# The first adapter's share of x: added to x tile by tile, instead of multiplied through W

## The reference

```
x1  = x  + (x @ B0[id0].T) @ A0[id0].T                      # first adapter
out = x1 + x1 @ W.T + b + 2 * ((x1 @ A1[id1]) @ B1[id1])    # base layer and second adapter
```

## Time and profile before

| what | value |
|---|---|
| median of 3 runs | 1397.52 us |
| profiled execution | 1398.88 us, its span 1396.9 us |
| TensorE busy | 1372.8 us, 98% |
| VectorE busy | 943.6 us, 68% |
| ScalarE busy | 529.1 us, 38% |
| moved by DMA | 311.6 MB, mean 223 GB/s |
| mean granted clock | 0.997 |

### The profile page before, as it was taken

The page is one execution under the profiler, slowest core; times in us unless marked ns, Lnnn a source line. Parts: engine busy times, 40 slices in busy tenths (PEclk is TensorE's granted clock), DMA queues, the critical chain, the costliest instruction groups (busy, mean ns, idle before and its releaser), DMA issues.

```text
span 1396.9 us, 16200 instructions
## 1 busy us (share of the span) xinstructions
PE 1372.8 (98%) x6024; PEld 1128.8 (81%) x6024; DVE 943.6 (68%) x1049; ACT 529.1 (38%) x588; POOL 79.1 (6%) x163
## 2 busy tenths in 40 slices
PE   6899999999999999999999999999999999999999
PEld 5788877888888878888888888888888888888887
DVE  4677897777877887687765566665755566665662
ACT  3444444433334443343324453333233444333321
POOL 2012010001010000001001000000101000000000
PEclk9999999999999999999999999999999999999999
DMA  9789764778888987599895335455856343555642
GB/s 343 242 293 306 264 238 147 243 236 282 297 292 307 314 297 264 178 301 327 287 358 194 110 112 180 163 175 168 276 204 189 117 135 134 169 167 189 194 151 83
DMA packets 98591, 311.60 MB, mean 223 GB/s; under 512 B 13009, under 2 KB 14289, under 8 KB 98513
## 3 DMA queue, kind: packets, MB, share of 16 engines
q1 hardware_dynamic: 92736, 298.96, 63.1%
q0 software_dynamic: 5776, 11.61, 2.9%
HBM read 254.94 MB, written 55.57 MB: 222 GB/s over the span
## 4 chain that ended last, share of the span: by engine, by line
PE 91%; DVE 4%; DMA 2%; issue 1%; ACT 1%; SPq 1%; ACTq 0%; DVEq 0%
PE acc L590 27%; PE acc L591 27%; PE acc L592 27%; DMA w_two<-w 2%; PE acc L565 2%; PE down_ps L549 2%; PE down_ps L550 2%; PE image_ps L535 1%; PE image_ps L529 1%; PE image_ps L530 1%; DVE w_one L759 1%; DVE bg_lo L794 1%; DVE w_lo L767 1%; DVE x_lo L789 0%; ACT w_hi L627 0%
## 5 line engine op out<-in xcount | busy, mean ns | idle before, releaser
L590 PE MATMUL acc<-x_hi,w_hi 128*128 128x512 f32 x1792 | 702.1, 392 | 16.3 <-DVE x_lo L789 12.5
L591 PE MATMUL acc<-x_lo,w_hi 128*128 128x512 f32 x1792 | 699.5, 390 | 0.0
L592 PE MATMUL acc<-x_hi,w_lo 128*128 128x512 f32 x1792 | 699.1, 390 | 0.0
L627 ACT ACTIVATE w_hi<-w_one 128x1024 fp32r<-128x1024 f32 x223 | 235.9, 1058 | 541.1 <-PE acc L592 504.5
L767 DVE TENSOR_TENSOR w_lo<-w_one,w_hi 128x1024 fp32r<-128x1024 f32 x223 | 273.1, 1225 | 215.2 <-ACT w_hi L627 215.2
L590 PEld LDWEIGHTS acc<-x_hi,w_hi 128*128 128x128 f32 x1792 | 337.6, 188 | 89.0 <-issue 16.6
L591 PEld LDWEIGHTS acc<-x_lo,w_hi 128*128 128x128 f32 x1792 | 337.6, 188 | 71.7 <-issue 1.0
L592 PEld LDWEIGHTS acc<-x_hi,w_lo 128*128 128x128 f32 x1792 | 337.3, 188 | 71.2
L660 ACT ACTIVATE sums<-acc 128x512 f32<-128x512 f32 x96 | 57.1, 594 | 203.7 <-PE acc L592 188.1
L826 DVE SCALAR_TENSOR_TENSOR sums<-acc,bias_sb,sums 128x512 f32<-128x512 f32 x128 | 95.7, 747 | 22.0 <-PE acc L565 20.8
L759 DVE TENSOR_TENSOR w_one<-w_one,w_two 128x1024 f32<-128x1024 f32 x79 | 96.4, 1220 | 17.1 <-DMA w_two<-w 17.1
(11 more groups left out here) (61 smaller groups left out, 610.3 us busy)
## 6 DMA issues: line engine op xcount, KB each, us to landing
w_one<-w SPq DMA_DIRECT2D x143, 512.0 KB, 5.5
w_one<-w_sums SPq DMA_DIRECT2D x80, 512.0 KB, 3.7
w_two<-w SPq DMA_DIRECT2D x79, 512.0 KB, 7.4
x_stage<-x SPq DMA_DIRECT2D x64, 512.0 KB, 4.4
out<-sums SPq DMA_DIRECT2D x128, 256.0 KB, 4.6
w_sums<-w_one SPq DMA_DIRECT2D x40, 512.0 KB, 4.1
resident<-x SPq DMA_DIRECT2D x32, 512.0 KB, 8.6
bg_raw<-w_rows SPq DMA_DIRECT2D x32, 512.0 KB, 5.0
```

What stands on the lines that cost most here:

```text
L590: pe.matmul(ps[:, :], w_hi[ws][:, c, :], hi, start=(c == 0), stop=False)
L591: pe.matmul(ps[:, :], w_hi[ws][:, c, :], lo, start=False, stop=False)
L592: mm = pe.matmul(ps[:, :], w_lo[ws][:, c, :], hi, start=False, stop=(c == H - 1))
L627: act.activation(w_hi[s % W_PARTS][:, :, :], w_one[s % W_ONES][:, :, :], ACT.Copy).then_inc(w_hi_ready, 1)
```

## The change

The image of W goes. In its place x1 = x + A0·(B0·x) is formed tile by tile, and all seven products work on x1.
- `project_down(d)`: B0·x and A1·x of a sample, as before, but in halves of a chunk (128 x 512) with three small buffers. Sample 1's eight chunks stand ahead of step 0, and sample 0's in steps 0 to 2. Those of the next group lie in products 4 and 5 of the group before.
- `project_up(v)`: two matmuls of 96 rows, with A0's columns (`up_w`, loaded and split by `load_up` and `split_up`) against `rank_x`, into two PSUM banks.
- `add_up(v)`: VectorE adds the banks to a chunk of x. Half of the chunks are in `resident`. The others are loaded to `bg_raw`, added, stored to a DRAM tensor `x1`, and read from there as operands.
- The product of A1, A0 and b1 is still needed for the second adapter, as its down part is taken of x and not of x1. Four matmuls with `across` (`make_image`, steps 6 to 9) form it.

The core of the diff (ScalarE's start has the order of VectorE's; lines left out are marked):

```diff
+def sum_at(p):
+    if p == 1:
+        return (5, 5, 6, 7)
+    return {1: (2, 3, 5, 6), 2: (2, 3, 6, 7)}.get(p % PRODUCTS, (1, 3, 5, 6))
...
+def downs(s):
     if s >= STEPS:
         return []
+    if s < 3:
+        first = (0, 8, 10, 13, 16)
+        return list(range(first[s + 1], first[s + 2]))
     g, i, o = where(s)
...
+    if g + 1 < GROUPS and H * 4 <= s % PER_GROUP < H * 5:
+        return [16 * (g + 1) + o]
+    if g + 1 < GROUPS and H * 5 < s % PER_GROUP <= H * 6:
+        return [16 * (g + 1) + 8 + s % PER_GROUP - H * 5 - 1]
+    return []
+def ups(s):
+    if s >= STEPS:
+        return []
+    if s < 0:
+        return [0, 1]
+    g, i, o = where(s)
+    found = [2, 3] if s == 0 else []
+    if i == 0:
+        found += [16 * g + 4 * A0 + r for r, at in enumerate((1, 2, 4, 5) if g else (4, 4, 5, 5)) if at == o]
+    found += [16 * g + 4 * B0 + r for r, at in enumerate((7, 8, 10, 11)) if at == s % PER_GROUP]
+    if i == 2:
+        found += [16 * g + 4 * A1 + r for r, at in enumerate((1, 3, 5, 7)) if at == o]
+    if i == 6 and g + 1 < GROUPS:
+        found += [16 * (g + 1) + r for r, at in enumerate((2, 4, 5, 6)) if at == o]
+    return found
...
+RANK_X_AT = {s + (1 if n < 2 else 2): n for s, n in LAST.items()}
...
+UP_SPLIT = {2: 1}
+UP_LOAD = {}
+for _g in range(GROUPS):
+    _s = PER_GROUP * _g
+    if _g:
+        UP_LOAD[_s - 15], UP_SPLIT[_s - 12] = 4 * _g + B1, 4 * _g + B1
+        UP_LOAD[_s - 7], UP_SPLIT[_s - 1] = 4 * _g + A0, 4 * _g + A0
+    UP_LOAD[_s + (3 if _g == 0 else 0)], UP_SPLIT[_s + 6] = 4 * _g + B0, 4 * _g + B0
+    UP_LOAD[_s + 7], UP_SPLIT[_s + 12] = 4 * _g + A1, 4 * _g + A1
+DOWN_AFTER = ((1, 3, 5), (5, 6))
+IMAGE_STEP = 6
...
+        up_w = sb("up_w", [96, D // 2], F32R)
+        rank_x = [sb(f"rank_x{k}", [96, T], F32R) for k in range(3)]
...
+        up_ps = [bank(f"up_ps{k}") for k in range(2)]
+        image_ps = bank("image_ps")
...
-                source = x_chunk(2 * g + 1, 0, r) if i < 4 else x_chunk(2 * g, 1, r)
+                y = RAW["up", 16 * g + 4 * (B0 if i < 4 else A1) + r]
+                sp.wait_ge(x1_stored[y % 2], DMA * raw_stores(y))
+                source = x1[2 * g + (i < 4)][:, 2 * r:2 * r + 2, :]
...
+            def load_raw(kind, number):
+                y = RAW[kind, number]
+                if y >= 2:
+                    before, one = RAW_AT[y - 2]
+                    if before == "down":
+                        sp.wait_ge(bg_ready, 2 * one + 2)
+                    else:
+                        sp.wait_ge(x1_stored[y % 2], DMA * raw_stores(y - 2))
...
+            def store_x1(v):
+                y = RAW["up", v]
+                n, half, r = up_chunk(v)
+                sp.wait_ge(up_added, 2 * v + 2)
+                sp.dma_start(x1[n][:, 2 * r:2 * r + 2, :], bg_raw[y % 2][:, :, :]).then_inc(x1_stored[y % 2], DMA)
...
+            for d in (0, 1):
+                load_raw("down", d)
+            for d in (2, 3):
+                load_early(d)
...
+            sp.wait_ge(ids_loaded, 2 * DMA)
+            sp.dma_start(down_raw[0][:, :, :], adapter(0, 1, b0).rearrange("u p c r -> (u p) c r")).then_inc(first_down_loaded, DMA)
+            sp.dma_start(down_raw[1][:, :, :], adapter(1, 1, a1).rearrange("u p c r -> (u p) c r")).then_inc(first_down_loaded, DMA)
+            for r in range(CH):
                 load_resident(0, 1, r)
+            sp.dma_start(identity_sb[:, :], identity).then_inc(identity_loaded, DMA)
+            load_w(0)
             load_w(1)
+            for r in range(CH):
+                load_resident(0, 0, r)
+            for d in (12, 13):
+                load_raw("down", d)
             load_w(2)
-            for r in range(2):
-                load_resident(0, 0, r)
+            keep_sum(0)
+            for d in (14, 15):
+                load_early(d)
...
+                for v in ups(s - 1) if s else ():
+                    if not up_resident(v):
+                        store_x1(v)
...
+                if s in (1, 2):
+                    for n in range(4 * s - 4, 4 * s):
+                        sp.dma_start(a1_raw[:, n, :, :], adapter(1, n, a1).rearrange("u p c r -> (u p) c r"))\
...
+                for v in ups(s + 1):
+                    if not up_resident(v):
+                        load_raw("up", v)
+                if s + 2 >= CH:
+                    for d in downs(s + 2):
+                        load_raw("down", d)
...
+            def project_down(d):
+                n, k = down_chunk(d)
                 if k == 0:
                     pe.wait_ge(down_ready, turn(n) + 1)
                     if turn(n):
                         pe.wait_ge(down_added, turn(n))
                 for u in range(2):
+                    pe.wait_ge(bg_ready, 2 * d + u + 1)
                     c = 2 * k + u
+                    hi, lo = down_parts(2 * d + u)
                     weights = down[:, c, :, :, :].rearrange("p h l r -> p (h l r)")
-                    pe.matmul(down_ps[:, :], weights, hi[:, u, :], start=(c == 0), stop=False)
-                    mm = pe.matmul(down_ps[:, :], weights, lo[:, u, :], start=False, stop=(c == C - 1))
-                mm.then_inc(bg_used, 1)
+                    pe.matmul(down_ps[:, :], weights, hi, start=(c == 0), stop=False)
+                    pe.matmul(down_ps[:, :], weights, lo, start=False, stop=(c == C - 1)).then_inc(bg_used, 1)
+            def project_up(v):
+                n, half, r = up_chunk(v)
+                if r == 0:
+                    pe.wait_ge(up_ready, v // 4 + 1)
+                    pe.wait_ge(rank_x_ready, turn(n) + 1)
+                for u in range(2):
+                    e = 2 * v + u
+                    if e >= 2:
+                        pe.wait_ge(up_added, e - 1)
+                    o = 2 * r + u
+                    pe.matmul(up_ps[e % 2][:, :], up_w[:, P * o:P * (o + 1)], rank_x_of(n)[:, :], start=True, stop=True)\
+                      .then_inc(up_done, 1)
+            def make_image(j):
+                pe.wait_ge(across_ready, 1)
+                pe.wait_ge(b1_rows_loaded, NB * DMA)
+                if j:
+                    pe.wait_ge(image_ready, j)
+                pe.matmul(image_ps[:, :], across, rows[:, T * j:T * (j + 1)], start=True, stop=True).then_inc(image_done, 1)
...
+                    if c == 1 and len(us) > 0:
+                        project_up(us[0])
                     if c == 3 and s >= 1:
                         add_rank(s - 1)
-                    if c == 5 and len(zs) > 1:
-                        multiply_chunk(zs[1])
-                    if c == 6 and len(zs) > 2:
-                        multiply_chunk(zs[2])
+                    if c == 3 and len(us) > 1:
+                        project_up(us[1])
+                    if c in DOWN_AFTER[s == 0]:
+                        k = DOWN_AFTER[s == 0].index(c)
+                        if k < len(ds):
+                            project_down(ds[k])
+                    if c == 6 and 0 <= s - IMAGE_STEP < 4:
+                        make_image(s - IMAGE_STEP)
+            for d in downs(-1):
+                project_down(d)
+            for v in ups(-1):
+                project_up(v)
...
+            def split_chunk(d):
+                wait_for_down_source(act, d)
+                for e in (2 * d, 2 * d + 1):
+                    if e >= 11:
+                        act.wait_ge(bg_used, e - 2)
+                    act.activation(down_parts(e)[0], down_source(e), ACT.Copy).then_inc(bg_hi_ready, 1)
+            def split_up(m):
+                act.wait_ge(up_loaded, 3 * DMA * (m + 1))
+                if m:
+                    act.wait_ge(up_done, 8 * m)
                 else:
...
+                    act.wait_ge(zeros_ready, 1)
+                for row in (0, 4 * R):
+                    act.activation(up_w[row:row + R, :], rank_raw[row:row + R, :], ACT.Copy)
+                act.activation(up_w[2 * R:3 * R, :], rank_raw[2 * R:3 * R, :], ACT.Copy).then_inc(up_hi_ready, 1)
...
+                    dve.wait_ge(up_added, up_number(p, r))
+                    if g == 0:
+                        dve.wait_ge(bg_ready, 32)
...
+            def split_chunk(d):
+                for e in (2 * d, 2 * d + 1):
+                    hi, lo = down_parts(e)
+                    dve.wait_ge(bg_hi_ready, e + 1)
+                    dve.tensor_tensor(lo, down_source(e), f32(hi), ALU.subtract).then_inc(bg_ready, 1)
...
+            def add_up(v):
+                n, half, r = up_chunk(v)
+                if up_resident(v):
+                    dve.wait_ge(resident_loaded[n % 2][r], DMA * (n // 2 + 1))
+                    chunk = resident[n % 2][:, 2 * r:2 * r + 2, :]
+                else:
+                    y = RAW["up", v]
+                    dve.wait_ge(bg_loaded[y % 2], DMA * raw_loads(y))
+                    chunk = bg_raw[y % 2][:, :, :]
+                for u in range(2):
+                    dve.wait_ge(up_done, 2 * v + u + 1)
```

(74 more changed lines are left out.)

402 lines of the change are left out of this document (168 added, 234 removed).

## The result

The changed kernel takes 1415.66 us (median of 4 runs, 1414.24 to 1420.35) against 1397.38: a ratio of 1.013 (95% interval 1.010 to 1.0161), 18.3 us slower. The profiled execution of it is the longest of the four, 1420.35, so its account adds up to more: a span of 1418.7 against 1396.9, +21.8. A second profile, of a run of 1412.27, is used where the two differ.

A forecast was written before the change was run, and what follows sets the result against it. TensorE, busy 98% of the span, was taken as the bound. Terms -15.3 + 22.1 + 2.3 - 3.2 + 4 + 4 = +13.9 on the profiled 1398.9 gave 1412.8, 1411 as a median; range 1396 to 1424.

The forecast's parts named there:

- TensorE's work: Whole kernel: image matmuls of 43.5 and 3.8 us go, up matmuls of 32.0 come: -15.3 us.
- start: Ahead of step 1: step 0 needs all of x[1] first; step 1 starts at 54, 37.5 lost for 15.4: +22.1 us.
- steps 1 to 16: TensorE waits for VectorE in steps 4, 5, 7 and 8: 10.2 us lost against 7.9, +2.3.
- product 2 and 3 of group 0: Forecast for product 2 of group 0: its chunks go, and their losses with them: -3.2 us.
- transfers, group 1: Product 1 of group 1: 18.9 MB in 45 us ask for about 420 GB/s, so W lags: +4 us, bounds 0 and +12.
- clock: Waits at the start and in steps 4 and 7 drop TensorE to 1.2 GHz: +4 us, bounds 0 and +9.
- One sign: Start: VectorE is busy without a gap from W(0)'s landing at about 20.
- The rival of a start held by transfers alone: Start +12, step 1 near 44, no new waits or clock and transfer costs: 1383 to 1390 us, chance 0.12.
- Steps 4 to 8: TensorE waits for up additions in steps 4 and 5 (3.9, 1.3), for image copies in 7 and 8 (3.7, 1.3).
- Its ceiling: Group 1, product 1: transfers capped at product 6's 354 GB/s, so 18.9 MB take 53.4 us, a lag of 8.4.
- lighter stretches follow: Group 1, behind product 1: asking for W ahead absorbs 3.5 us of the 8.4 lag, and lighter stretches come next.
- The rule of the Trainium skill: Each of five waits (start, steps 4, 5, 7, 8) costs 3.4 us, 17 for 4: 1424, chance 0.06.

The follow-up runs named there:

- The start's order: Changed kernel with VectorE and ScalarE splitting all eight chunks of x[1] before W(0), and add_up between x_hi and x_lo: 1410.83 us.
- the run with the clock held up: Changed kernel with extra matmuls of zeros in TensorE's waits at the start, in step 0 and in step 4: 1414.37 us.
- the queue order: Changed kernel with the image copy right behind w_lo in VectorE's list, and in steps 4 and 5 the first add_up there too: 1407.97 us.
- the second timing: The changed kernel as it is, timed again beside the kernel before: 1414.31 us, ratio 1.0114.

## Why the prediction was right

| term of the sum | predicted | profile after | second profile |
|---|---|---|---|
| TensorE's work | -15.3 | -15.5 | -15.4 |
| start | +22.1 | +25.3 | +24.2 |
| steps 1 to 16 | +2.3 | +4.3 | +3.1 |
| product 2 and 3 of group 0 | -3.2 | -3.2 | -3.2 |
| transfers, group 1 | +4 | +10.9 | +5.0 |
| clock | +4 | in the start and steps 1 to 16 | same |

The lost time before is 15.4 at the start, 7.9 in steps 1 to 16 and 2.4 in group 1; each entry but the first is the loss after less that. TensorE's work is what the other rows leave of +21.8 and of +13.7 (span 1410.6).

- **TensorE's work** came as counted: 5928 records for 6024, steps of 5.44 or 5.69 plus 0.25 for each up matmul from step 10 on, and 335.5 us for group 2 with its 32 up matmuls, 327.6 before. The gain is real and smaller than what was paid for it.
- **The start**: right in mechanism, 3.2 short for step 1 (57.2 for 54). Step 0 started at 39.1 for 37.8, W(0)'s sum at 19.97 for 20.2, and chunks came every 3.6 for 3.7. The rest is the low clock in step 0 (2.4 of the first profile's 3.2), priced in the clock's line. One sign failed: VectorE was to be busy without a gap from 20 on, but is busy 3.9 us of 25 to 30, since ScalarE waits 2.47 for a split buffer. The prediction had no such wait: 32 down matmuls, the first of them at the low clock, stood between ScalarE and its buffers. The start's order proved a part of the cause (3 to 5 us); mended, that wait was next, and no order found got step 1 below 48. The rival of a start held by transfers alone (step 1 near 44) did not come.
- **Steps 4 to 8**: 3.9, 1.3, 3.7, 1.3 predicted, 5.7, 1.1, 3.4, 1.2 found. Only step 4 was off in the first profile, where the clock fell to 0.77 in 85 to 90, and 4.1 in the second. Moving the instructions halved the loss, as the reason said. But the waits were not all where the prediction put them: in step 4 1.4 us stand ahead of the first up part, which it priced at nothing, and only 1.9 ahead of the second; in step 7 1.3 are the up weights and 1.6 the copy. That the sums of 3.9 and 3.7 came so near is partly luck.
- **Product 2 of group 0**: right.
- **Transfers**: the mechanism was right and the term mis-sized, 10.9 and 5.0 for 4. Its ceiling was wrong: 354 GB/s was what product 6 asked for, not what can be had. Product 1 moved 386 at a share of 1.01 and lost only 1.4 (391 and nothing in the second profile). At 386 its 18.9 MB take 49.0, 3.6 more than its 45.4 of work, an estimate close to the 3.5 that loads asked for ahead were to absorb. The loss came one product later than worked out, in product 2, as the lag was handed on in W loads that land late; the step "lighter stretches follow" failed there. By the Trainium skill (HBM Reference, Specifications) 425 GB/s would have been open and nothing lost; no product with stores in it reached more than 394 here, and the loss was there.
- **The clock**: right in mechanism, and not steady in size. Against the run with the clock held up, step 5 starts 3.6 later in the first profile and 1.3 in the second, for 4 predicted. Low clock and lost time are the same only where TensorE sets the pace: in step 4 of the kernel before it did (2.9 us), at that kernel's start it didn't. The rule of the Trainium skill (TensorE: Matmul & The Clock Gate, HAM oscillation) that every long gap is followed by a slow stretch held at the start, where the clock was 0.50 to 0.53 in three stretches; behind step 7's waits of 1.3 and 1.6 it stayed at 1.00, and in the profile of the queue order it did so behind the 3.25 as well (1.00 in 50 to 55). As a rule for the time it would have been far off.
- **The sum**: 13.9 predicted, 13.7 in the second profile, 21.8 in the first, 18.3 between the medians (15.5 in the second timing). In the second profile the start, steps 1 to 16 and the clock together are 27.3 for 28.4, and the transfers 5.0 for 4. In the first they are 29.6 and 10.9, so the transfers make most of the excess. The sign and the range came from the terms; that the sum came within 5 us of the median depends on which executions were timed.

## What to carry to other kernels

Count what a change puts ahead of the first matmul that matters, in the order of the busiest engine's queue: 15 us of matmuls saved along the kernel weighed less than 25 us more of start, in which no product could run. Before pricing a low clock or a wait, ask whether the engine is the bound in that stretch, and price one stretch at a time. Product 1 of group 1 stood at a share of 0.91; four loads and four stores more brought it to 1.01, and the loss showed one product later. So look at the stage behind a full one too.

## What the runs showed of the hardware

Loads and stores mixed moved 386 to 394 GB/s at a share of 1.01 to 1.02 (product 1 of group 1 in four profiles), more than the 354 at 0.99 that looked like the ceiling before, so here a share near 1 did not give the ceiling of another mix. A matmul of 96 rows cost 0.25 where one of 128 costs 0.227. The same wait of 3.25 ahead of the same matmul was followed by the low clock in one execution (the next matmuls 0.43 to 0.56 apart) and by the full clock in another (0.23 to 0.31 apart). The same program differed by 8 us between executions (1412.3 and 1420.4), 5.9 of it in group 1, where the transfers are full; the kernel before stayed within 4.3 over 21 runs.
